# Full-height bias products, a low part on GpSimd and a product kept in PSUM, in a graph and feed-forward block

## The reference, cut to what matters

```python
xn = layernorm(x)
x  = x + (segment_sum(w[:, None] * xn[src], dst) @ Wg + bg)        # graph part
x  = x + linear_attention(xn)       # q, k = elu(xn @ W + b) + 1, 8 heads; out @ Wp + bp
z  = layernorm(x)
g  = mean over the rows of (relu(z @ G1.T + c1) @ G2.T + c2)       # 8 gate values
W1m, b1m, W2m, b2m = W1, b1, W2, b2 each + sum over e of g[e] * tv_e
h   = relu(z @ W1m.T + b1m)                                        # 256 hidden columns
res = z + h @ W2m.T + b2m
out = x + (res - mean) * rsqrt(var + eps) * lng + lnb
```

## Time and profile before

| | |
|---|---|
| median of 3 runs | 1598.65 us (1595.19 to 1599.21) |
| profiled execution | 1604.54 us, its span 1602.7 us |
| mean granted TensorE clock | 0.946 |
| TensorE busy | 1385.1 us, 86% |
| VectorE busy | 1015.7 us, 63% |
| ScalarE busy | 648.3 us, 40% |
| GpSimd busy | 843.4 us, 53% |
| DMA | 366.46 MB, mean 229 GB/s |

### The profile page before, as it was taken

How to read it: one execution, slowest core, us unless ns; L and a number is a source line. 1 busy time by engine, 2 the same in 40 slices (tenths; PEclk the granted TensorE clock), 3 DMA queues, 4 the chain that set the end, 5 groups by cost and what they waited for, 6 DMA issues and landing times. The chain is left out here.

```text
span 1602.7 us, 24972 instructions
## 1 busy us (share of the span) xinstructions
PE 1385.1 (86%) x7963; PEld 605.9 (38%) x7963; DVE 1015.7 (63%) x2041; ACT 648.3 (40%) x1045; POOL 843.4 (53%) x882
## 2 busy tenths in 40 slices
PE   4988978898889888998898988998995998889893
PEld 2544423333333333333333433433342443633331
DVE  7978634344343434385666667877878675448997
ACT  4787722222222322033333323333333665256663
POOL 0001267777777777477777777777771000033432
PEclk9999989999999999699999999999997999899996
DMA  6989678888888888477777777777777879514432
GB/s 214 312 310 341 242 247 274 272 267 271 261 260 274 268 267 290 138 238 237 230 237 236 237 229 234 240 242 250 230 224 183 220 197 223 158 60 151 157 138 85
DMA packets 201553, 366.46 MB, mean 229 GB/s; under 512 B 77101, under 2 KB 82879, under 8 KB 201441
## 3 DMA queue, kind: packets, MB, share of 16 engines
q0 software_dynamic: 62720, 205.57, 41.9%
q1 hardware_dynamic: 138000, 158.43, 30.7%
q10 hardware_dynamic: 720, 1.06, 0.2%
HBM read 287.93 MB, written 65.38 MB: 220 GB/s over the span
## 5 line engine op out<-in xcount | busy, mean ns | idle before, releaser
L1165 POOL DMA_INDIRECT rows<-y_rows,idxT x516 | 492.4, 954 | 184.6 <-issue 165.7
L919 ACT ACTIVATE mb<-bank,ones,ncols 128x512 f32<-128x512 f32 x98 | 76.3, 779 | 445.8 <-PE bank L1964 445.8
L1519 DVE SCALAR_TENSOR_TENSOR acc<-bank,maskt,acc 128x512 f32 x196 | 138.0, 746 | 102.3 <-PE bank L2072 81.9
L2060 PE MATMUL bank<-rows,hots 128*32 128x512 f16 x1548 | 118.1, 412 | 55.5 <-DMA rows<-y_rows,idxT 47.2
L1964 PE MATMUL bank<-Wg,xtb 128*128 128x512 f16 x588 | 139.1, 388 | 16.1 <-DVE xtb L1453 8.9
L1964 PE MATMUL bank<-ztg,G 128*128 128x512 f16 (+1 forms) x624 | 130.7, 371 | 15.5 <-DMA ztg<-zhigh 14.1
L1964 PE MATMUL bank<-KVP,qT 128*128 128x512 f16 x588 | 143.9, 397 | 0.0
L1964 PE MATMUL bank<-Wk,xta 128*128 128x512 f16 x588 | 139.5, 388 | 0.0
L1964 PE MATMUL bank<-Wq,xta 128*128 128x512 f16 x588 | 139.2, 388 | 0.0
L1200 POOL TENSOR_TENSOR acc<-acc,lnbb 128x512 f32 (+1 forms) x49 | 66.0, 1349 | 116.4 <-ACT zq L1051 116.4
L2044 PE MATMUL bank<-xr,kh 128*128 128x512 f16 x392 | 123.7, 399 | 2.4 <-DVE kl L1546 2.4
(11 more groups left out here) (311 smaller groups left out, 2428.9 us busy)
## 6 DMA issues: line engine op xcount, KB each, us to landing
xta<-xt_rows SPq DMA_DIRECT2D x98, 256.0 KB
x_rows<-xhl SPq DMA_DIRECT2D x49, 256.0 KB, 3.8
xt_rows<-xtb SPq DMA_DIRECT2D x49, 256.0 KB, 3.9
y_rows<-yb SPq DMA_DIRECT2D x49, 256.0 KB, 3.6
xr<-x_rows SPq DMA_DIRECT2D x49, 256.0 KB
zt_rows<-ztg SPq DMA_DIRECT2D x49, 256.0 KB, 2.3
acc<-in_x SPq DMA_DIRECT2D x48, 256.0 KB, 4.2
xd<-zt_rows SPq DMA_DIRECT2D x12, 1024.0 KB, 5.4
```

The lines of the kernel that those rows point to most:

```text
L919: nc.scalar.activation(mb[:, :], of[:, :], ACT.Relu, scale=ncols[:, col:col + 1], bias=ones[:, 0:1]).then_inc(f_min, 1)
L1165: pool.indirect_dma_start(out=row_slot(s, k).rearrange("p a d -> p (a d)"), out_offset=None, in_=y_rows, in_offset=bass.IndirectOffsetOnAx ...
L1519: nc.vector.scalar_tensor_tensor(out=flat(acc, tile + m), in0=edge_bank(n)[:, :], scalar=maskt[:, m, n:n + 1], in1=flat(acc, tile + m), op ...
L2060: ins = nc.tensor.matmul(edge_bank(n)[W * k:W * k + W, :], hots[:, r, p, :, hot_column(s, k)], row_slot(s, k)[:, q, :], start=s == FIRST[n ...
```

## The change

- `ones3`, `krows` and `qrows` become 128 rows high. GpSimd clears the last two at the start (two memsets more, so the counts of `pool_set` that are waited for rise by two), and the three real rows are filled as before; `scale3` is made over all 128 rows. The bias products of keys, queries and last pass are then 128 rows high, with zeros in 125 of them.
- The scale of the relu rows is folded into two columns ahead of the pass (`cols[:, 7:8]`, `b1m[:, FC:]`). From quad 1 on ScalarE's relu makes scaled rows, its second instruction is a plain copy to float16, and the low part, h32 minus the high part, is a subtraction on GpSimd (`hidden_rest`), behind `add_base` in ticks 0 and 1 of a quad. VectorE's `hidden_low` remains for quad 0 alone.
- `gain` writes to PSUM bank 6 in the place of `cen`, and `finish` reads it there.

The diff, cut to its core:

```diff
@@ -206,7 +206,7 @@
         ones = put("ones", [P, P], F32)
-        ones3 = put("ones3", [3, P], BF16)
+        ones3 = put("ones3", [P, P], BF16)
         headmask = put("headmask", [P, P], F32)
@@ -245,8 +245,8 @@
         flag = put("flag", [1, 1], I32)
-        krows = put("krows", [3, D], BF16)
-        qrows = put("qrows", [3, D], BF16)
+        krows = put("krows", [P, D], BF16)
+        qrows = put("qrows", [P, D], BF16)
         rM = cursor[0]
@@ -316,9 +316,9 @@
         tvW1 = over(rA, ("tvW1", [P, NE, FC, D], F32))
-        xd, hT, zq, cen, squares = over(
+        xd, hT, zq, squares = over(
             rA, ("xd", [P, 2, Q4, 2, C, P], F16), ("hT", [P, 2, 2, FC, D], F16), ("zq", [P, 2, D], F32),
-            ("cen", [P, D], F32), ("squares", [P, D], F32))
+            ("squares", [P, D], F32))
         G16, ztg = over(rP, ("G16", [P, 2, C, D], F16), ("ztg", [P, 2, Q4, 2, C, P], F16))
@@ -332,7 +332,7 @@
             ("gbr", [1, NE], F32), ("b1c", [P, FC], F32), ("tvb1", [P, FC, NE], F32),
-            ("b1m", [P, FC], F32), ("tvb2", [NE, D], F32), ("geye", [P, NE, P], F32))
+            ("b1m", [P, 2 * FC], F32), ("tvb2", [NE, D], F32), ("geye", [P, NE, P], F32))
         (W1raw, W2raw, lnrows, lbrows, g2raw, lngb, lnbb, lncoef, gjunk, gsum, gsq, gcol, gbias, g2T,
@@ -957,7 +957,7 @@
             act.wait_ge(y_low, T)
-            act.wait_ge(pool_set, 20)
+            act.wait_ge(pool_set, 22)
             for s in range(K_FIRST, SLOTS_END):
@@ -1036,12 +1036,12 @@
                         act.wait_ge(o_done, Q4 * (q - 1))
-                    at_least(act, low_made, H_LOW + FC * (q - 1) + o + 1)
-                    nc.scalar.activation(h32[:, o, 0:n], bank[2 + o][:, 0:n], ACT.Relu, scale=cols[:, 1:2],
-                                         bias=b1m[:, o:o + 1]).then_inc(high_made, 1)
+                    first = isinstance(q, int) and q == 1
+                    at_least(act, low_made, H_LOW + FC if first else H_LOW + FC * (q - 1) + o + 1)
+                    nc.scalar.activation(h32[:, o, 0:n], bank[2 + o][:, 0:n], ACT.Relu, scale=cols[:, 7:8],
+                                         bias=b1m[:, FC + o:FC + o + 1]).then_inc(high_made, 1)
                     act.wait_ge(high_made, H_HIGH + FC * q + o + 1)
-                    nc.scalar.activation(hT[:, par, 0, o, 0:n], h32[:, o, 0:n], ACT.Copy, scale=scf[:, 2:3]
-                                         ).then_inc(h_out, 1)
+                    nc.scalar.copy(hT[:, par, 0, o, 0:n], h32[:, o, 0:n]).then_inc(h_out, 1)

@@ -1091,6 +1091,8 @@
             pool.memset(headmask[:, :], 0.0).then_inc(pool_set, 1)
+            pool.memset(krows[:, :], 0.0).then_inc(pool_set, 1)
+            pool.memset(qrows[:, :], 0.0).then_inc(pool_set, 1)
             pool.memset(epsc[:, :], EPS).then_inc(pool_set, 1)
@@ -1103,14 +1105,14 @@
                       allow_small_or_imprecise_dtypes=True).then_inc(pool_set, 1)
-            pool.wait_ge(pool_set, 15)
+            pool.wait_ge(pool_set, 17)
             for m in (ident, ident16):
...
                                    pattern=[[-1, P]], channel_multiplier=1).then_inc(pool_set, 1)
-            pool.wait_ge(pool_set, 17)
+            pool.wait_ge(pool_set, 19)
             for b in range(2):
                 pool.memset(headmask[b * HD:(b + 1) * HD, b * HD:(b + 1) * HD], 1.0).then_inc(pool_set, 1)
-            pool.wait_ge(pool_set, 19)
+            pool.wait_ge(pool_set, 21)
             pool.nop(nofuse=True).then_inc(consts_made, 1)
@@ -1192,6 +1194,16 @@

+            def hidden_rest(g, j):
+
+                quad = quad_at(g, j)
+                if j % Q4 < FC and not (isinstance(quad, int) and quad + 1 >= NQ):
+                    par, n, o = (j // Q4 + 1) % 2, P if isinstance(quad, int) and quad + 1 == NQ - 1 else Q4 * P, j % Q4
+                    pool.wait_ge(h_out, FC * (quad + 1) + o + 1)
+                    waited(pool)
+                    nc.gpsimd.tensor_tensor(hT[:, par, 1, o, 0:n], h32[:, o, 0:n], hT[:, par, 0, o, 0:n], ALU.subtract
+                                            ).then_inc(low_made, 1)
+
             def add_base(g, j):
@@ -1199,7 +1211,11 @@

-            row_ticks(pool, add_base, T)
+            def last_tick(g, j):
+                add_base(g, j)
+                hidden_rest(g, j)
+
+            row_ticks(pool, last_tick, T)

@@ -1861,6 +1877,8 @@
             powers(2, 1, link)
+            link(nc.vector.tensor_scalar(cols[:, 7:8], cols[:, 1:2], scf[:, 2:3], None, ALU.mult))
+            link(nc.vector.tensor_scalar(b1m[:, FC:], b1m[:, 0:FC], scf[:, 2:3], None, ALU.mult))
             dve.nop(nofuse=True).then_inc(scales_made, 1)
@@ -1887,7 +1905,7 @@
             link(nc.vector.tensor_tensor(cols[:, 5:6], scf[:, 2:3], scf[:, 3:4], ALU.mult))
-            link(nc.vector.tensor_scalar(scale3[:, 0:P], ones3[:, :], cols[0:3, 5:6], None, ALU.mult))
+            link(nc.vector.tensor_scalar(scale3[:, 0:P], ones3[:, :], cols[:, 5:6], None, ALU.mult))

@@ -1925,7 +1943,7 @@
                     at_least(dve, ob_made, t5)
-                    nc.vector.scalar_tensor_tensor(out=cen[:, :], in0=res[:, j5, :], scalar=negm[:, par5, i5:i5 + 1],
+                    nc.vector.scalar_tensor_tensor(out=bank[6][:, :], in0=res[:, j5, :], scalar=negm[:, par5, i5:i5 + 1],
                                                    in1=lngb[:, :], op0=ALU.add, op1=ALU.mult).then_inc(gained, 1)
@@ -1935,7 +1953,7 @@
                     waited(dve)
-                    nc.vector.scalar_tensor_tensor(out=ob[:, b5, :], in0=cen[:, :], scalar=rsr[:, par5, i5:i5 + 1],
+                    nc.vector.scalar_tensor_tensor(out=ob[:, b5, :], in0=bank[6][:, :], scalar=rsr[:, par5, i5:i5 + 1],
                                                    in1=flat(acc, t5), op0=ALU.mult, op1=ALU.add).then_inc(ob_made, 1)
@@ -1949,9 +1967,6 @@
                     finish(gn, jn)
-                if j % Q4 in (1, 2) and not (isinstance(quad, int) and quad + 1 >= NQ):
-                    hidden_low(quad + 1, (j // Q4 + 1) % 2, P if isinstance(quad, int) and quad + 1 == NQ - 1 else Q4 * P,
-                               [j % Q4 - 1])
             row_ticks(dve, out_tick, T + 2)
...
```

More of the change, by code:

```diff
@@ L1670, in tile_at_group @@
                 return dve.value_load(tileof[0:1, n:n + 1], min_val=0, max_val=T - 2)
-            dve.wait_ge(pool_set, 20)
+            dve.wait_ge(pool_set, 22)
             for s in range(K_FIRST, SLOTS_END):
@@ L1836, in _ @@
                 link(nc.vector.tensor_tensor(tvb1[:, o, :], tvb1[:, o, :], gall[:, :], ALU.mult))
-            link(nc.vector.tensor_reduce(b1m[:, :], tvb1[:, :, :], AX_X, ALU.add))
-            link(nc.vector.tensor_tensor(b1m[:, :], b1m[:, :], b1c[:, :], ALU.add))
-            link(nc.vector.tensor_reduce(mx[:, 4:5], b1m[:, :], AX_X, ALU.max, apply_absolute_value=True))
+            link(nc.vector.tensor_reduce(b1m[:, 0:FC], tvb1[:, :, :], AX_X, ALU.add))
+            link(nc.vector.tensor_tensor(b1m[:, 0:FC], b1m[:, 0:FC], b1c[:, :], ALU.add))
+            link(nc.vector.tensor_reduce(mx[:, 4:5], b1m[:, 0:FC], AX_X, ALU.max, apply_absolute_value=True))
             merge_w2(0)
```

## The result

The median of the changed kernel is 1572.72 us (4 runs, 1569.67 to 1576.55), against 1596.92 us (4 runs, 1594.09 to 1599.21) for the kernel before beside it: ratio 0.985, 95% interval 0.9826 to 0.9875. The forecast was 1574.5. The profiled execution took 1572.78 us with a span of 1570.8. Beside the experiments on one chip, one execution of the kernel before took 1781.46 us at a granted clock of 0.745, and it enters no ratio.

A forecast was written before the change was run, and what follows sets the result against it. VectorE was taken to bound the last pass, TensorE close behind, and GpSimd's gathers the edge stage. Start 1.4, quads 18.3 and tail 4.5 make 24.2 us off the median 1598.65, giving 1574.5; range 1561 to 1588.

The forecast's parts named there:

- The sum: Last pass: 1.4 us from its start, 18.3 from nine quads, 4.5 from the tail, together 24.2 us.
- The padding's price: TensorE's bias products: each change of operand height costs about 0.105 us, so 0.21 a product, 0.84 a quad.
- Rival 1: Padding of the bias products does nothing; a quad takes 12.3 us, the kernel 1581; chance 0.12.
- The cover of the key and query products: Gather stage: 98 bias products, 20.6 us of TensorE time, count 0 under GpSimd's 1.25 us step.
- Rival 3: Key and query stages gain too because TensorE ends them, up to 20.6 us: 1557 to 1568; chance 0.08.
- The low part in time: Last pass: GpSimd's subtraction, taken as 1.3 us, lands with 2.4 us to spare, so TensorE's wait goes.
- one of my signs of being wrong: The forecast is wrong if TensorE then waits for GpSimd; no size given.
- The quad: Last pass: a quad falls from 13.73 to 11.7 us, TensorE bounding with VectorE next to it; bounds 11.2 and 12.8.
- The upper bound: Last pass: a quad of 12.8 us, called half of the way to a collision in every tick (13.4).
- the first operation's collisions: Last pass: VectorE's first operation still reads two SBUF tiles; excess from GpSimd rises from 0.27 to 0.4 us a tile.
- Rival 2: Last pass slower through the lock between GpSimd and VectorE, quad 16.4 us, kernel 1625; chance 0.05.
- a plain shift of 5.9: Whole kernel: the median lies 5.9 us below the profiled execution, so 1580.3 becomes 1574.5.

The follow-up runs named there:

- a_pad64: The full change, but bias operands 64 rows high in place of 128; 1578.52 us, ratio 0.9893 to the kernel before.
- pad_last: The full change, but key and query bias products read only 3 rows, those of the last pass stay 128; 1571.56 us, ratio 0.9853.
- d_norm: The full change plus the norm weights copied once into PSUM bank 7 for the first operation; 1569.73 us, ratio 0.9825.
- b_pool: The kernel before with only the low part of the relu rows moved to GpSimd; 1586.26 us, ratio 0.9945.
- c_psum: The kernel before with only the product kept in PSUM; 1592.11 us, ratio 0.9982.
- ab: The full change with the product put back in SBUF, so padding and low part on GpSimd; 1586.57 us, ratio 0.9941.
- bc: The full change with 3-row bias products, so low part on GpSimd and product in PSUM; 1572.32 us, ratio 0.985.
- P: The padding of the bias products to 128 rows; alone on the kernel before 1594.02 us, ratio 0.999.
- G: The low part of the relu rows on GpSimd; alone on the kernel before 1586.26 us, ratio 0.9945.
- S: The product kept in PSUM; alone on the kernel before 1592.11 us, ratio 0.9982.

## Why the prediction was right

- **The sum.** 24.2 us were forecast for the pass and 25.1 came: start 1.1 (1.4 forecast), quads 19.1 (18.3), tail 4.9 (4.5). The median moved by 24.2 against the runs beside it.
- **The padding's price.** 0.21 us for a bias product was right in its cause (`a_pad64`) and nearly in its size: 0.76 us over the 4 of a quad where TensorE alone decides (12.05 against 11.29), so 0.19 each. In the start I counted 7 products. The residual of tile 5, which ends it, waits for six, and the first one's leading side lies ahead of it: 11 changes of height at 0.105 are 1.15, and 1.1 came. Rival 1 (it does nothing) falls. The Trainium skill, "TensorE: Matmul & The Clock Gate", LDWEIGHTS, from which that rival came, says that the number of rows does not matter to a load; the loads of 3 rows take 90 to 91 ns and those of 128 rows 96 to 98, so it agrees as far as the load goes; the starts of the products disagree with its use for the whole.
- **The cover of the key and query products.** Right (`pad_last`). Rival 3 falls.
- **The low part in time.** Right for the waits: none is left for VectorE's low part. GpSimd's subtraction is 1.16 us in the median, against 1.3 taken. A wait of TensorE for GpSimd was one of my signs of being wrong, and one came: the weight load of a bias product at 1546.11 waited 2.76 us for GpSimd's low part. It lies in the tail, where VectorE sets the pace, and is the only one in the pass.
- **The quad.** 11.61 against 11.7, bounds 11.2 and 12.8. TensorE's floor of 11.2 is 11.29 in `d_norm`. The upper bound was called half of the way to 13.4, which from 11.7 would be 12.55; and rival 3's lower end should be 1554 (1574.5 less 20.6), not 1557. Neither touches the forecast.
- **The mis-sized term: the first operation's collisions.** I raised its excess from 0.27 to 0.40 a tile, because GpSimd works more, and said its mean stays over 1000. It is 979 (0.23). In its place GpSimd got longer, 1349 to 1432 an addition; GpSimd is busy 71.1 of the 104.5 us of the quads. `b_pool` shows the same of that step alone: GpSimd works half as much again, and the first operation's mean goes from 1020 to 1027 only. The one kernel where it rises by more than 10 ns is `c_psum` (1105), and there GpSimd has no more work than before, so how often the two meet depends on more than GpSimd's load. Rival 2 (the lock makes it slower) had the mechanism but not the size.
- **What I had no step for.** Between a quad of 11.61 and one of 11.29 lie 2.9 us over the nine, and most of it is a wait for the load of xd. In the chain of waits of the kernel after, the load is issued only after a final operation has made `ob`, and takes 5.6 us to land; in the timeline TensorE then stands for it:

```profile
1493.87 0.76 DVE ob L1956
1494.79 0.33 SPq L798
1495.40 5.60 DMA xd<-zt_rows
```
```profile
1501.13 1.03 PE L1979 MATMUL bank<-xd,W1m 128*128 128x512 f16 x4 [0.32 <-DMA xd<-zt_rows]
```

These waits come to 2.1 us in four; they are 11.6 in `ab`. In `d_norm` they are gone, but also in `bc`, whose final operations are no shorter; that the load comes in time because the final operations come earlier is my reading.
- **The parts don't add.** Alone P, G and S take 3.2, 10.9 and 4.3 us off the pass, 18.4 in all; together 25.1. What one is worth depends on which others stand: P takes 3.2 us off alone, 2.4 behind G, 9.6 behind S, 4.1 behind both; G 10.9, 10.0 behind P, 16.7 behind S, 11.2 behind both; S 4.3, 10.7 behind P, 10.2 behind G, 11.9 behind both. Of P's four steps only the one behind S shows in the time (0.9982 to 0.9895, intervals apart). The forecast took the quad for all three at once, from the work left to each engine, so this did not disturb it; the prices of single parts that I expected afterwards for P alone, S alone and P with S were off.
- **Luck.** The profiled span fell by 31.9, not 24.2; I had tied the forecast to the medians and not to that long execution, by a plain shift of 5.9, and that held. That the medians moved by just the 24.2 of the sum is luck: the pass fell by 25.1, and in `bc` the median moved by 24.7 while the pass fell by 21.0. It could have come out some us to either side.

**Open.** Why the 4.1 us that the padding takes off the pass (`bc` against after) don't show in the median. The padded key and query products may give some back: the gathers' stretch less stalls is 990.9 to 994.0 us in the profiles that have them and 989.3 to 991.2 in those that don't. But `pad_last` and the full change have the same median, so the runs don't show it either. Against it stands `a_pad64`: its pass is that of `bc` (156.0 and 156.2 us) and its median, on the same chip, 6.2 us longer, with 993.9 against 991.0 us of gathers less stalls and 7.4 against 3.9 us in the two longest stalls. Its key and query products have 64 rows, those of `bc` 3; nothing more was tried. TensorE's clock around 655 us, which differed between the profiles together with the stall, wasn't varied.

## What to carry to other kernels

Read an accumulating product's cost from start to start, and give a small bias product the height of its neighbours; but ask first what else is late, for alone this was worth nothing that could be measured, and behind the product kept in PSUM 9.6 us. When two engines are within some per cent of each other, take work off both together, and don't judge a part by doing it alone: undo it in the final kernel too. Where VectorE and GpSimd run side by side, look at the means of VectorE's operations with two SBUF operands: a constant operand copied once into a free PSUM bank took every collision of these operations away.

## What the runs showed of the hardware

- A product of 3 or of 64 rows between products of 128 adds 0.11 us at each of its two sides (0.32 start to start against 0.21, 512 columns, granted clock 1.00). At 128 rows nothing is added, also from f16 to bf16 and back.
- VectorE's 128x512 operation with two f32 operands in SBUF takes 858 to 1105 ns on the mean beside GpSimd; with one of them in PSUM 743 to 751, whatever GpSimd does. The loss is shared: the addition takes 1269 to 1282 ns where both the first and the final operation have an operand in PSUM, and 1347 to 1567 elsewhere. The Trainium skill, "SBUF — State Buffer", Who interferes with whom, has the two engines share one pair of ports under an exclusive lock, which VectorE needs for a second SBUF operand or in a two-port mode; these means agree with it for the second operand, and no run here tries the modes.
- A subtraction of f32 and f16 into f16, 128x512, takes GpSimd 1.16 us in `d_norm` (median; 1.164 at most), less than its f32 addition (1.27), and up to 1.61 where it collides (`b_pool`).
